# Two reordered fronts, early first expert pairs, and one block per layer in a macaron block with top-2 experts

## The chip, the cores and the metric

The kernel runs on one core of a Trainium2 chip. The time is the device time in microseconds (us) from the first to the last instruction of one execution. Five engines work side by side: TensorE (PE; its weight loads are PEld), VectorE (DVE), ScalarE (ACT), GpSimd (POOL) and SyncE (SP). Each takes its own instructions strictly in order and waits on semaphores; transfers run on 16 DMA engines, and SP, ACT and POOL issue them. Execution of a wait blocks everything behind it on the same engine.

## The reference, cut to what matters

Input x has 8 x 1024 tokens of 128 features in float32. Twice a layer of experts is applied with half weight, and attention stands between:

```python
x = x + 0.5 * ffn(layernorm(x))        # layer 0
x = x + attn(layernorm(x))             # linear attention, 16 heads of 8
x = x + 0.5 * ffn(layernorm(x))        # layer 1, the same weights

# ffn(xf): 16 experts, 2 of them for each token, and 1 shared one
scores = softmax(xf @ gate_w + gate_b)
top_vals, top_idx = top_k(scores, 2)
cw = (one_hot(top_idx, 16) * top_vals[..., None]).sum(axis=1)
a = silu(xf @ w1 + b1) * (xf @ w3 + b3)              # per expert, 128 -> 176
y = einsum('teh,ehd,te->td', a, w2, cw) + cw @ b2
z = silu(xf @ sw1 + sb1) * (xf @ sw3 + sb3) @ sw2 + sb2   # shared, 128 -> 352

# attn(xf)
q, k, v = xf @ Wq + bq, xf @ Wk + bk, xf @ Wv + bv   # split into heads
q, k = elu(q) + 1, elu(k) + 1
kv = einsum('bhnd,bhnf->bhdf', k, v)
out = einsum('bhnd,bhdf->bhnf', q, kv) @ Wp + bp
```

## The kernel before

The 8192 tokens are 64 tiles of 128 rows. A *group* is 8 tiles (1024 tokens), a *chunk* is 4 tiles (512 tokens), so there are 8 groups and 16 chunks. The residual stays in SBUF as `xa`. Five phases follow each other: front 0, experts 0, front 1, experts 1, combine. Each is one block of five engine programs and ends in `phase`, which clears its semaphores and makes all engines meet.

**A front** (`front`, n = 0 or 1) does for each group: layer norm (DVE `moments`, `variances`; the scale on DVE in front 0, on POOL in front 1; ACT `rows`), transposes on PE (`turn`) copied by ACT (`turned`), the gate's matmuls (`gating_mm`), the top two on DVE (`largest`, `indices`, `hot`), a count on PE with triangular ones (`count`), and from it on DVE each token's slot in its expert's region (`places`). POOL then sends each tile's normalised rows to the DRAM array `xs` by one indirect DMA a tile: `first(c)` for the first choice of a chunk, and after DVE has rewritten the row's tail (`rewrite(c)`, which waits until these sends have landed, `sent0`), `second_choice(c)`. Beside it runs the shared expert, six parts m for each group: PE `ups(m)` (6 matmuls of 512 columns), ACT `silus(m)`, DVE `gates(m)`, PE `downs(m)`, and per chunk DVE `outs`. PE's `ups(0)` needs the split weights `sw13l`, which DVE makes. Front 0 also splits the 16 experts' weights into a high and a low part through one PSUM buffer `p_w`: PE `weight_mean(e)`, ACT `weight_high(e)`, DVE `weight_low(e)`. Front 1 first adds what the experts wrote (`residual`, from `yt` loaded by SP) and does the attention (`attention`, `phi_q`, `phi_k`, `attended`) two groups ahead of the shared expert. Near the end `tables`, `table` and `tables_out` make the list of expert tiles, and SP copies 16 padding tiles.

The order of the work is written out by hand: `step(s)` in front 0 and `step_1(s)` in front 1 on each engine, with an `opening` in front 1. In front 0 the start was `step(-1)` and `step(0)`.

**The experts** (`experts`) take 72 pairs of tiles. SP loads pair j into `xin[j % 8]` once the slot's old rows are sent; for pair j PE transposes (`p_x`), multiplies with the two experts' weights (`p_u`), transposes `a` (`p_a`) and multiplies with `w2` (`p_y`); DVE scales into `y`, and POOL sends it to the DRAM array `ys` with two indirect DMAs a pair. PE's step j holds: transposes of pair j+1, up of pair j, transposes of `a` of pair j-1, down of pair j-2.

**Combine** adds `ys` to `xa` in 8 pieces of 1 MB (4 buffers) and stores 8 pieces of 0.5 MB.

```python
        front(nc, k, sb, ps, 0, xa, xs_dram, w)
        experts(nc, k, sb, ps, 0, xs_dram, ys_dram)
        front(nc, k, sb, ps, 1, xa, xs_dram, ys=ys_v)
        experts(nc, k, sb, ps, 1, xs_dram, ys_dram)
        combine(nc, sb, xa, ys_v, out_v)
```

## Time and profile before

| | us |
|---|---|
| median of 3 runs | 942.99 (941.9 to 943.26) |
| profiled execution | 942.32 |
| its span, first to last instruction | 940.6 |
| PE busy | 785.1 (83%) |
| DVE busy | 580.3 (62%) |
| POOL busy | 568.9 (60%) |
| ACT busy | 470.5 (50%) |
| mean granted TensorE clock, share of full | 0.94 |

The span outside the instructions is 942.32 - 940.6 = 1.7 us. In the trace front 0 runs from 0 to 215 us, experts 0 to 416, front 1 to 702, experts 1 to 905, and combine to the end. A row of the timeline reads: start in us, duration in us, engine, line of the kernel, operation, what it writes <- what it reads, how often, and in brackets how long its engine had stood idle and which engine, tile and line released it. "SPq" and "ACTq" are issues of DMAs by that engine.

### The profile page before, as it was taken

How to read it: one execution, taken by the hardware profiler on the slowest of the kernel's cores; microseconds unless marked ns; L12 is line 12 of the kernel's file. 1: busy time of each engine (PE TensorE's matmuls, PEld its weight loads, DVE VectorE, ACT ScalarE, POOL GpSimd, SP SyncE). 2: the span in 40 equal slices, each digit the busy share in tenths (PEclk: the TensorE clock that was granted, in tenths of full speed). 3: DMA queues.
4: the chain of work that ended last, by engine and by line, in shares of the span. 5: the costliest groups of instructions: out<-in, count | busy, mean ns of one | idle time of the engine just before them, and what ended most of it. 6: DMA issues, size and time to landing. Idle time of an engine off the chain costs nothing. (4 is left out here: it accounts for less than half of the span.)

```text
span 940.6 us, 20435 instructions
## 1 busy us (share of the span) xinstructions
PE 785.1 (83%) x5348; PEld 699.7 (74%) x5349; DVE 580.3 (62%) x2146; ACT 470.5 (50%) x968; POOL 568.9 (60%) x585
## 2 busy tenths in 40 slices
PE   2899999886999999936678999999868999999910
PEld 2577777666999999934567777787758999999900
DVE  7688786643555555537667877766634555555535
ACT  2465566423555555525457667675314555555500
POOL 1376777772777776751167667765643777776730
PEclk9999999997999999977889999999798999999965
DMA  9921221132333333324112211111133333333349
GB/s 279 157 65 55 70 70 59 52 98 66 102 101 101 104 101 101 100 97 145 65 32 83 76 39 46 35 38 35 43 81 81 108 101 104 101 101 98 93 185 376
DMA packets 83816, 90.45 MB, mean 96 GB/s; under 512 B 20391, under 2 KB 69421, under 8 KB 82733
## 3 DMA queue, kind: packets, MB, share of 16 engines
q1 hardware_dynamic: 64046, 45.41, 19.1%
q0 software_dynamic: 17408, 35.95, 11.4%
q10 hardware_dynamic: 2304, 8.39, 2.3%
q8 instruction: 27, 0.44, 0.2%
q14 instruction: 31, 0.25, 0.1%
HBM read 47.45 MB, written 44.37 MB: 98 GB/s over the span
## 5 line engine op out<-in xcount | busy, mean ns | idle before, releaser
L1415 POOL DMA_INDIRECT ys<-e_y,e_x x288 | 276.6, 960 | 134.4 <-issue 88.7
L354 POOL DMA_INDIRECT xs<-f_xrow,f_slot x256 | 261.1, 1020 | 128.0 <-issue 74.6
L1534 PE MATMUL e_py<-w,e_at 97*128 (+1 forms) x1152 | 152.1, 274 | 0.0
L1534 PEld LDWEIGHTS e_py<-w,e_at 97*128 97x128 f32 (+1 forms) x1152 | 139.9, 191 | 0.1
L1439 DVE TENSOR_TENSOR e_a<-e_pu,e_sil 128x352 f32<-128x352 f32 x144 | 75.6, 525 | 97.6 <-ACT e_sil L1465 97.6
L1446 DVE TENSOR_SCALAR e_y<-e_py,e_x 128x128 f32<-128x128 f32 x288 | 87.8, 347 | 57.6 <-PE e_py L1534 57.3
L1168 PEld LDWEIGHTS f_pz<-sw,f_gated 128*128 128x128 f32 (+1 forms) x768 | 101.6, 195 | 14.3 <-DVE f_gated L561 4.5
L1465 ACT ACTIVATE e_sil<-e_pu 128x352 f32<-128x352 f32 x144 | 67.0, 465 | 90.3 <-PE e_pu L1511 90.3
L1509 PE MATMUL e_pu<-w13h,e_xth 128*128 x288 | 107.2, 372 | 0.0
L1459 ACT ACTIVATE e_xth<-e_px 128x256 fp32r<-128x256 f32 x144 | 55.6, 386 | 101.0 <-PE e_px L1498 101.0
L1168 PE MATMUL f_pz<-sw,f_gated 128*128 128x128 f32 (+1 forms) x768 | 103.4, 279 | 3.0 <-DVE xa L571 2.9
L946 ACT ACTIVATE f_sil<-f_phg,sb 128x512 f32<-128x512 f32 (+1 forms) x96 | 65.3, 686 | 78.9 <-PE f_phg L1154 74.7
L561 DVE SCALAR_TENSOR_TENSOR f_gated<-f_phg,sb,f_sil 128x512 f32<-128x512 f32 (+1 forms) x96 | 71.5, 746 | 41.2 <-ACT f_sil L946 35.6
L1154 PE MATMUL f_phg<-f_xth,sw13h 128*128 128x512 f32 (+1 forms) x192 | 88.1, 459 | 8.4 <-ACT f_sil L946 6.4
L1510 PE MATMUL e_pu<-w13l,e_xth 128*128 x288 | 94.3, 327 | 0.0
L1511 PE MATMUL e_pu<-w13h,e_xtl 128*128 x288 | 94.2, 327 | 0.0
L1471 ACT ACTIVATE e_at<-e_pa 96x512 f32<-96x512 f32 x144 | 85.8, 596 | 1.6 <-PE e_pa L1521 1.6
L1521 PE MATMUL e_pa<-ident,e_a 128*96 128x128 f32 x576 | 86.2, 272 | 0.0
L1154 PE MATMUL f_phg<-f_xtl,sw13h 128*128 128x512 f32 (+1 forms) x192 | 77.6, 404 | 0.0
L1154 PE MATMUL f_phg<-f_xth,sw13l 128*128 128x512 f32 (+1 forms) x192 | 77.6, 404 | 0.0
L1498 PE MATMUL e_px<-ident,e_x 128*128 128x128 f32 x288 | 57.7, 282 | 21.2 <-DMA e_x<-xs 17.0
L1521 PEld LDWEIGHTS e_pa<-ident,e_a 128*96 128x96 f32 x576 | 67.2, 125 | 5.1
(168 smaller groups left out, 1320.2 us busy)
## 6 DMA issues: line engine op xcount, KB each, us to landing
e_x<-xs SPq DMA_DIRECT2D x288, 65.0 KB
f_yt<-ys SPq DMA_DIRECT2D x16, 512.0 KB, 4.1
c_yt<-ys SPq DMA_DIRECT2D x8, 1024.0 KB, 10.4
ys<-e_y,e_x POOLq DMA_INDIRECT x288
xa<-in_attn_x ACTq DMA_DIRECT2D x8, 512.0 KB, 9.8
xs<-f_xrow,f_slot POOLq DMA_INDIRECT x256, 2.4
out<-xa ACTq DMA_DIRECT2D x8, 512.0 KB
f_raw<-in_ffn_w SPq DMA_DIRECT2D x32, 88.0 KB
```

The costliest lines, as they stand in the source:

```text
L354: pool.indirect_dma_start(xs, bass.IndirectOffsetOnAxis(slot[:, q, i:i + 1], 0), xrow[:, i, :], None).then_inc(done, 16)
L1154: last = pe.matmul(p_hg[(2 * m + g) % NH][0:wd], w_[:, cols], x_[c % NX][:], start=q == 0, stop=q == 2)
L1168: last = pe.matmul(p_z[c % NZ][:, tok], gated[c % 2][0:wd, f, tok], k.sw2[0:wd, f], start=f == 0 and q == 0, stop=f == 2, skip_group_check ...
L1415: pool.indirect_dma_start(ys, bass.IndirectOffsetOnAxis(xin[r][:, t, D:D + 1].bitcast(I32), 0), y[r][:, t, :], None).then_inc(sent[r], 16)
L1439: dve.tensor_tensor(a[r][:], p_u[r][:, :, INTER:UP], sil[r][:], ALU.mult).then_inc(aa, 1)
L1446: last = dve.tensor_scalar(y[s][:, t], p_y[j % 2][:, t * D:(t + 1) * D], xin[s][:, t, D + 1:D + 2], None, ALU.mult)
L1471: act.activation(at[r][0:A0], p_a[0:A0], ACT.Copy).then_inc(turned, 1)
L1509: pe.matmul(o, xth[r][:, tok], k.w13h[:, cols], start=True, stop=False)
L1510: pe.matmul(o, xth[r][:, tok], k.w13l[:, cols], start=False, stop=False)
L1511: last = pe.matmul(o, xtl[r][:, tok], k.w13h[:, cols], start=False, stop=True)
L1521: last = pe.transpose(p_a[0:A0, q * P:(q + 1) * P], a[r][:, t, o:o + A0], k.ident[:])
L1534: last = pe.matmul(p_y[r][:, t * D:(t + 1) * D], at[r][0:rows_, q], w2, start=c == 0, stop=c == 1, skip_group_check=True)
```

## The change

1. The front and the experts of a layer are one block without a clearing and a meeting of the engines in between. Each engine goes on by itself, and waits for `ended`: all `outs` done, all sends landed, the table made (and in layer 0 the attention's weights). SP loads the first 4 pairs as soon as pads and sends have landed, before the other conditions. At the end of the experts SP loads the first 4 chunks of `ys` before the engines meet. The buffers of these loads, `k.xin` and `k.yt`, are now allocated for the whole program, and front 0's raw weights and front 1's `xt_a` lie in them.
2. Front 0 begins with an order of its own instead of `step(-1)` and `step(0)`. The odd experts' weight splits move from the end of step s to the second part of step s+1. `rewrite(2(s-1))` moves ahead of `gates(m + 1)`, `tables` behind `low`. SP, not ACT, loads the tokens of groups 3 to 7. ACT runs one early exponential on a constant.
3. Front 1: `phi_k` ahead of the two shifts in `features`, ACT's `exps(0)` behind `turned_a(5)`, and the count of step 7 one part later.
4. Experts: the down projection and the weighing of pair 0 stand at the end of step 1 instead of step 2.
5. Combine works in 16 chunks with 12 buffers.

```diff
+def load_x(nc, sp, k, n, xin, xs, first, pairs, free=None, turn=None):
+    _, at = nc.values_load_multi_w_load_instructions(
+        k.tile_at[0:1, ds(first, 2 * len(pairs))], engines=[mybir.EngineType.SP],
...
+    for q, r in enumerate(pairs):
+        if free is not None:
+            sp.wait_ge(free[r], turn)
+        for t in range(2):
+            sp.dma_start(xin[r][:, t], slot_rows(xs)[:, ds(at[2 * q + t], 1)].rearrange(
+                "p j c -> p (j c)")).then_inc(k.x_in[n][r], 16)
+def layer(nc, k, sb, ps, n, xa, xs, ys, ys_v, w=None):
+    with phase(nc) as sem:
+        with ExitStack() as ctx:
+            first, ended = front(nc, k, sb, ps, sem, ctx, n, xa, xs, w, ys_v)
+        with ExitStack() as ctx:
+            second = experts(nc, k, sb, ps, sem, ctx, n, xs, ys, ys_v, ended)
+            with nc.Block(no_gpsimd_drain=True) as block:
+                @block.sync
+                def _(sp):
+                    first[0](sp)
+                    second[0](sp)
...
@@ front, SP @@
             load_expert(3)
+            for g in range(3, GROUPS):
+                load_tokens(sp, g)
...
         sp.wait_ge(pads, 16 * E)
+        sp.wait_ge(sent1, 16 * TILES)
+        load_x(nc, sp, k, n, [k.xin[:, r] for r in range(AHEAD)], xs, 0, range(AHEAD))
...
@@ front 0, DVE step(s) @@
-                    gates(m + 1)
-                    outs(2 * (s - 1) - 1)
             rewrite(2 * (s - 1))
-                    gates(m + 2)
             if s == 1:
                 rewrite(1)
+            gates(m + 1)
+            if s <= GROUPS:
+                weight_low(2 * s - 1)
+            outs(2 * (s - 1) - 1)
+            gates(m + 2)
...
@@ front 1, DVE features(a) @@
             phi_q(a, 1)
+            phi_k(a, 0)
+            phi_k(a, 1)
             shifts(a - 1)
             shifts_a(a + 1)
-                    phi_k(a, 0)
-                    phi_k(a, 1)
...
@@ front 0, DVE after the memsets @@
-                    step(0)
+            largest(0)
+            indices(0)
+            hot(0)
+            sums(0)
+            places(0)
+            low(0)
+            low(1)
             dve.wait_ge(swhi, 1)
             dve.tensor_tensor(k.sw13l[:], raws[:], k.sw13h[:].bitcast(F32), ALU.subtract
                               ).then_inc(swlo, 1)
+            weight_low(0)
+            moments(2)
+            variances(2)
+            scales(2)
...
@@ front 1, ACT opening @@
             rows_a(4)
-                    exps(0)
-                    rows_a(5)
             turned_a(4)
-                    high(0)
+            rows_a(5)
             turned_a(5)
+            exps(0)
+            high(0)
             high(1)
...
@@ front 0, ACT start @@
-                    step(-1)
-                    step(0)
+            for c in range(2):
+                rows(c)
+                turned(c)
+            rows(2)
+            rows(3)
+            turned(2)
+            exps(0)
+            turned(3)
+            high(0)
+            high(1)
             act.wait_ge(sw_in, 32)
...
@@ front 0, PE step(s) @@
                 ups(m)
+                if i == 1 and n == 0 and s <= GROUPS:
+                    weight_mean(2 * s - 1)
                 downs(m - 2)
...
-                            if gating and n == 0:
-                                weight_mean(2 * s + 1)
...
@@ front 1, PE step_1(s) @@
-                        if i == (1 if s == 1 else 0) and gating:
+                if i == (1 if s in (1, GROUPS - 1) else 0) and gating:
                     count(s)
...
+    ended = [(outr, CHUNKS), (sent1, 16 * TILES), (tab_done, 1)]
+    if n == 0:
+        ended += [(bias, 2)]
...
@@ experts, SP @@
+        for done, value in ended:
+            sp.wait_ge(done, value)
+        load_x(nc, sp, k, n, xin, xs, 2 * AHEAD, range(AHEAD, RING))
         with sp.Fori(1, PAIRS // RING) as i:
...
+        for r in range(RING):
+            sp.wait_ge(sent[r], 32 * (PAIRS // RING))
+        for c in range(4):
+            load_y(sp, ys_v, c, k.yt[:, c], k.y_in[n][c])
...
@@ experts, PE step(j) (DVE the same with weigh) @@
-                    if 2 <= j:
+            if j == 1:
+                down_projection(2, 2)
+            if j > 2:
+                down_projection(j, jv)
...
@@ combine, SP @@
+                for c in range(4, CHUNKS):
+                    wait(sp, ysum, c - 11)
+                    load_y(sp, ys, c, yt[c % 12], in_ready[c])
```

Three places show how the rows of an engine's program move. First PE at the start of front 0, before (`f_pt` are transposes, `f_pg` the gate's matmuls and the count, `f_pw` a weight split, `f_phg` the first `ups`):

```order
L1132 MATMUL f_pt<-ident,f_xrow 128x128 x8
L1108 MATMUL f_pg<-gw_s,f_xt 128x16 x8
L1118 MATMUL f_pg<-f_mask,tri 128x128
...
L1176 MATMUL f_pw<-f_raw,f_centre 128x352
L1177 MATMUL f_pw<-f_rawb,f_part 128x352
L1132 MATMUL f_pt<-ident,f_xrow 128x128 x8
L1176 MATMUL f_pw<-f_raw,f_centre 128x352
L1177 MATMUL f_pw<-f_rawb,f_part 128x352
L1108 MATMUL f_pg<-gw_s,f_xt 128x16 x8
L1154 MATMUL f_phg<-f_xth,sw13h 128x512
```

and after:

```order
L1215 MATMUL f_pt<-ident,f_xrow 128x128 x8
L1191 MATMUL f_pg<-gw_s,f_xt 128x16 x8
L1215 MATMUL f_pt<-ident,f_xrow 128x128 x8
L1201 MATMUL f_pg<-f_mask,tri 128x128
...
L1259 MATMUL f_pw<-yt,f_centre 128x352
L1260 MATMUL f_pw<-yt,f_part 128x352
L1191 MATMUL f_pg<-gw_s,f_xt 128x16 x8
L1237 MATMUL f_phg<-f_xth,sw13h 128x512
```

The second eight transposes stand ahead of the count, and one weight split is gone from here. Second DVE in front 1's opening, before (`f_phq` and `f_phk` are `phi_q` and `phi_k`, `f_nm` and `f_nma` the two shifts, `xa<-xa,f_yt` the residual):

```order
L605 TENSOR_SCALAR f_vea<-f_mva 128x8
L617 SCALAR_TENSOR_TENSOR f_phq<-f_phq,f_phg 128x512 x2
L464 SCALAR_TENSOR_TENSOR f_nm<-f_mv,f_rs 128x8
L611 SCALAR_TENSOR_TENSOR f_nma<-f_mva,f_rsa 128x8
L622 SCALAR_TENSOR_TENSOR f_phk<-f_phk,f_phg 128x256 x2
L579 TENSOR_TENSOR xa<-xa,f_yt 128x512
```

and after:

```order
L671 TENSOR_SCALAR f_vea<-f_mva 128x8
L683 SCALAR_TENSOR_TENSOR f_phq<-f_phq,f_phg 128x512 x2
L688 SCALAR_TENSOR_TENSOR f_phk<-f_phk,f_phg 128x256 x2
L530 SCALAR_TENSOR_TENSOR f_nm<-f_mv,f_rs 128x8
L677 SCALAR_TENSOR_TENSOR f_nma<-f_mva,f_rsa 128x8
L645 TENSOR_TENSOR xa<-xa,yt 128x512
```

The two `f_phk` now stand ahead of the shifts, which need POOL's results. Third PE at the first pairs of the experts, before (`e_px` transposes of x, `e_pu` up, `e_pa` transposes of a, `e_py` down):

```order
L1511 MATMUL e_pu<-w13h,e_xtl 128x352
L1521 MATMUL e_pa<-ident,e_a 96x128 x4
L1498 MATMUL e_px<-ident,e_x 128x128 x2
...
L1511 MATMUL e_pu<-w13h,e_xtl 128x352
L1521 MATMUL e_pa<-ident,e_a 96x128 x4
L1534 ISA
L1534 MATMUL e_py<-w,e_at 128x128
```

and after:

```order
L1600 MATMUL e_pu<-w13h,e_xtl 128x352
L1610 MATMUL e_pa<-ident,e_a 96x128 x4
L1628 ISA
L1628 MATMUL e_py<-w,e_at 128x128
...
L1587 MATMUL e_px<-ident,xin 128x128 x2
```

The down projection of pair 0 follows the first transposes of `a` at once, ahead of the transposes and the up part of later pairs.

## Rows read from the trace of the kernel before

**Rows 1.** Stretches by --windows: engine busy us (instructions), PE clock, DMA share, GB/s.
```profile
472.00:701.00 229.00, 209.93 (x1300) 173.99 (x1300) 158.50 (x686) 137.75 (x282) 147.91 (x139) 0.96 0.17 52
908.00:935.00 27.00, 0.00 (x0) 0.00 (x0) 17.60 (x15) 0.00 (x0) 0.00 (x0) 0.50 1.00 410
```

**Rows 2.** Timeline of front 0's start, PE and DVE.
```profile
24.55 0.69 PE L1121 MATMUL f_pg<-f_mask,onesb 128*128 128x128 bf16 x8
...
29.15 0.28 DVE L516 TENSOR_TENSOR f_spot<-f_pg,f_base 128x128 f32<-128x128 f32 x1
...
30.93 1.45 DVE L550 TENSOR_TENSOR f_xtl<-f_xt,f_xth 128x512 fp32r<-128x512 f32 x2
...
35.05 0.89 DVE L885 TENSOR_TENSOR sw13l<-f_raws,sw13h 128x704 fp32r<-128x704 f32 x1 [0.15 <-ACT sw13h L1086]
...
36.00 3.59 PE L1108 MATMUL f_pg<-gw_s,f_xt 128*128 128x16 f32 x16 [2.16 <-DVE sw13l L885]
...
39.63 0.29 DVE L471 TENSOR_TENSOR f_lgt<-f_pg,gb_s 128x128 f32<-128x128 f32 x1 [3.61 <-PE f_pg L1108]
...
43.64 0.75 DVE L561 SCALAR_TENSOR_TENSOR f_gated<-f_phg,sb,f_sil 128x512 f32<-128x512 f32 x1 [1.08 <-ACT f_sil L946]
```

**Rows 3.** Timeline of front 0's steps: PE and POOL.
```profile
78.32 2.46 POOL L354 DMA_INDIRECT xs<-f_xrow,f_slot  x1 [5.29 <-DVE f_slot L532]
...
78.88 0.83 PE L1176 MATMUL f_pw<-f_raw,f_centre 128*128 128x352 f32 x2 [1.04 <-DVE w13l L642]
...
211.02 0.96 POOL L354 DMA_INDIRECT xs<-f_xrow,f_slot  x1 [0.30 <-issue]
```

**Rows 4.** The page's DMA issues: the sends of a front, median us to landing.
```profile
xs<-f_xrow,f_slot POOLq DMA_INDIRECT x256, 2.4
```

**Rows 5.** Timeline, SP's first loads for experts 0.
```profile
215.88 8.16 SPq L1402 DMA_DIRECT2D e_x<-xs  x16
```

**Rows 6.** Timeline of the first pairs of experts 0.
```profile
220.85 0.49 PE L1510 MATMUL e_pu<-w13l,e_xth 128*128 x1
...
225.12 0.59 ACT L1471 ACTIVATE e_at<-e_pa 96x512 f32<-96x512 f32 x1
...
226.56 1.06 PE L1534 MATMUL e_py<-w,e_at 97*128 x8
...
229.18 0.96 POOL L1415 DMA_INDIRECT ys<-e_y,e_x  x1 [17.20 <-DVE e_y L1446]
```

**Rows 7.** The page's groups: the same matmul over both experts' phases.
```profile
L1510 PE MATMUL e_pu<-w13l,e_xth 128*128 x288 | 94.3, 327 | 0.0
```

**Rows 8.** Timeline from experts 0 to front 1.
```profile
414.58 0.96 POOL L1415 DMA_INDIRECT ys<-e_y,e_x  x1 [0.30 <-DMA ys<-e_y,e_x]
417.86 27.91 SPq L297 DMA_DIRECT2D f_yt<-ys  x10
```

**Rows 9.** Timeline of front 1's opening, DVE and PE.
```profile
454.54 0.17 DVE L611 SCALAR_TENSOR_TENSOR f_nma<-f_mva,f_rsa 128x8 f32<-128x8 f32 x1 [1.29 <-POOL f_rsa L381]
...
455.09 1.22 PE L1246 MATMUL f_pb<-f_phk,f_v 128*128 128x128 f32 x4 [4.51 <-DVE f_phk L622]
```

**Rows 10.** Timeline of front 1's step 7.
```profile
665.90 0.29 PE L1118 MATMUL f_pg<-f_mask,tri 128*128 128x128 bf16 x1 [2.00 <-DVE f_mask L504]
...
669.54 0.75 DVE L561 SCALAR_TENSOR_TENSOR f_gated<-f_phg,sb,f_sil 128x512 f32<-128x512 f32 x1 [2.70 <-PE f_phg L1154]
```

**Rows 11.** Timeline from front 1 to experts 1.
```profile
695.50 0.96 POOL L354 DMA_INDIRECT xs<-f_xrow,f_slot  x1 [0.30 <-issue]
...
700.72 0.69 DVE L571 SCALAR_TENSOR_TENSOR xa<-f_pz,xa 128x512 f32<-128x512 f32 x1 [1.87 <-PE f_pz L1168]
...
704.31 9.39 SPq L1402 DMA_DIRECT2D e_x<-xs  x16
706.82 0.69 PE L1498 MATMUL e_px<-ident,e_x 128*128 128x128 f32 x2 [6.15 <-DMA e_x<-xs]
```

**Rows 12.** Timeline, the last addition of combine.
```profile
935.77 1.23 DVE L1574 TENSOR_TENSOR xa<-xa,c_yt 128x1024 f32<-128x1024 f32 x1
```

More of the change, by code:

```diff
@@ L50 @@
 RING = 8
+AHEAD = 4
 SENT_EARLY = 3
@@ L1552, in combine @@
-def combine(nc, sb, rs, ys, out):
-    with phase(nc) as sem, ExitStack() as ctx:
-        yt = [sb(f"c_yt{r}", [P, GT, 2 * D], ctx=ctx) for r in range(4)]
-        in_ready = [sem(f"c_in{r}") for r in range(GROUPS)]
+            gates(m)
+            if attending:
+                moments(f)
+            gates(m + 1)
+            if attending:
+                variances(f)
+            outs(2 * (s - 1) - 1)
+            if gating:
+                sums(s)
+                places(s)
+            if s == GROUPS - 1:
+                tables()
@@ new lines, in step_1 @@
+            if gating:
+                low(2 * s + 1)
+        if n == 0:
+            for r in range(4):
+                dve.memset(rawb[r][:], 0.0)
+            dve.memset(k.w2[0:32, 1], 0.0)
+            dve.memset(rawp[:], 0.0)
+            dve.memset(rowq[:], 0.0).then_inc(zeroed, 1)
+            moments(0)
+            variances(0)
+            scales(0)
+            shifts(0)
+            moments(1)
+            variances(1)
+            scales(1)
+            shifts(1)
+        for r in range(2):
+            dve.memset(gated[r][96:97, 2], 1.0)
@@ L1557, in combine @@
+def combine(nc, k, sb, rs, ys, out):
+    with phase(nc) as sem, ExitStack() as ctx:
+        yt = [k.yt[:, c] for c in range(4)]
+        yt += [sb(f"c_yt{r}", [P, CHUNK, 2 * D], ctx=ctx)[:] for r in range(8)]
+        in_ready = k.y_in[1] + [sem(f"c_in{c}") for c in range(4, CHUNKS)]
         half, ysum, stored = sem("c_half"), sem("c_ysum"), sem("c_stored")
```

2568 lines of the change are left out of this document (1278 added, 1290 removed).

## The prediction

> **What bounds the kernel now.** I read the share of busy time first, then the timeline around each phase's two ends, then who waits for whom inside a phase. Three things are to be seen. In the experts POOL sets the pace: from its first send to its last it needs 414.58 - 229.18 = 185.4 us for 143 intervals, 1.30 us each, of which 0.96 is the send and 0.30 the gap behind it [rows 6, 8]. In front 0 POOL is as near the bound as PE: it waits 5.29 us for the slots of group 2 at 78.32 [rows 3], and from there to 211.02 its 99 intervals take 132.7 us, 1.34 each or 21.4 a group of 16 sends, with hardly a wait. In front 1 PE is the bound, busy 209.93 of 229 us [rows 1]. Combine is bound by the DMA engines: share 1.00 at 410 GB/s [rows 1]. Between these phases nothing runs but landings, meetings and loads: 215.88 - 211.98 = 3.9 us from the end of POOL's last send of front 0 to the experts' first load [rows 3, 5], and 706.82 - 701.41 = 5.4 us from DVE's last work to PE's first at the second front's end [rows 11].
>
> The sum is made against the profiled execution of 942.32 us (span 940.6, 1.7 outside it), which is 0.7 below the median of 942.99.
>
> **Front 0, its start: -4.9.** PE's first full step begins at 36.00, released by DVE's `sw13l` (35.05 + 0.89 = 35.94) [rows 2]. In the new order DVE has only this between the end of the count (24.55 + 0.69 = 25.24) and `sw13l`: `places`, which takes 1.4 of the 1.8 us from 29.15 to 30.93 (the rest is a weight split), `low` for two chunks 1.45, and `sw13l` 0.89: 25.24 + 1.4 + 1.45 + 0.89 = 29.0. ACT and PE keep up in my count: the four transposes and copies end by 24.1, `high` and `sw13h` by 26. So PE starts its step 6.9 earlier. Not all of it carries. DVE now does a weight split (0.5) and moments, variances and scale of group 2 (about 4.6; most of what lay between 24.3 and 29.15) before the top two of group 1, so that these start at 34.1 and not 39.63, and the first `gates` behind ACT's silu come at 38.2 and not 43.64: -5.45. From there `weight_mean(2s-1)`, 1.6 us of PE (two rows of 0.8 as at 78.88 [rows 3]), stands between `ups(m+1)` and `ups(m+2)`, ahead of the count and the slots. It takes back up to 1.6 in each step, and PE's wait of 1.04 at 78.88 goes with the split that made it, as does DVE's work for that split. The two nearly cancel: no gain a step, and POOL's 21.4 stay the measure. Slots of group 2 come 4.5 to 5 earlier, and POOL from its send at 78.32 needs 211.02 - 78.32 us whatever PE does. Hence -4.9, with ends 0 (POOL gives it back) and -8 (7 waits of about 1.0 are gained too, until POOL's own pace stops it). Cover that could go: `rewrite(2(s-1))` now waits for sends that land 2.4 us after their issue [rows 4], before `gates(m+1)`. Four sends at 1.27 and the landing put it 7.6 us behind POOL's first send of the group, and the rest of DVE's step to the next slots is some 12 us by my count of its instructions: 20.4 with the 0.8 to POOL's start, less than POOL's 21.4, so it costs nothing; were it 2 us more, each of six steps would lose 1. The moved token loads cost nothing: group 3's are wanted near 40 us.
>
> **From front 0 to experts 0: -1.8.** The last send lands at 211.02 + 2.4 = 213.4 [rows 3, 4], and SP's first load goes out at 215.88 [rows 5]. The clearing, the meeting and 16 register loads lie between, 2.5 us. With SP waiting for the landing alone and loading 8 registers, I leave 0.6 to 0.7. That is -1.8; ends: -0.8 (register loads take the full 1.0 and more) and -2.5.
>
> **The first pairs: +0.7, twice.** PE runs without a gap here. The down part of pair 0 now waits for ACT's copy, which ends at 225.12 + 0.59 = 225.71, some 0.75 us after PE's transposes; before, PE used that time for pair 2 and came to it at 226.56 [rows 6]. So `y` of pair 0 is ready 0.8 earlier, and everything from pair 1 on 0.75 later. POOL, back to back from 229.18, starts 0.8 earlier but then waits for pair 1. PE, without a gap and at POOL's pace, does not catch up. I take +0.7 each; ends -0.8 (the early start is kept) and +0.8.
>
> **From the experts on: -0.8, twice.** 417.86 - (414.58 + 2.4) = 0.9 us lie between the last landing and the first load of `ys` [rows 8]; SP now loads right behind the landing. The trace shows no landing for these sends; I use the front's 2.4 [rows 4]. The same holds before combine. Ends 0 and -1.3 each.
>
> **Front 1: -1.4 and -2.4.** In the opening DVE waits 1.29 us for POOL's scale at 454.54, ahead of `phi_k`, and PE stands 4.51 us for `phi_k` [rows 9]. Moved ahead, `phi_k` starts 1.4 earlier, and the chain behind it (attention, moments, top two) has no gap to swallow that. What ACT's `exps(0)` frees for PE ends in DVE, which is busy: 0 more. In step 7 PE stands 2.00 us for the mask at 665.90, and then DVE 2.70 for `ups(37)` [rows 10]. The six matmuls now fill PE's wait. The count comes 1.5 to 2 us later but still ahead of `gates(37)`: -2.4 for the slots of group 7, on which POOL, the rewrites and the tail hang. Ends: 0 and -6.
>
> **From front 1 to experts 1: -5.3, and -1.5 for the clock.** DVE's last `outs` ends at 701.41, PE's first expert matmul starts at 706.82 [rows 11]. The last send of this front lands at 695.50 + 2.4 = 697.9, so the first load goes out at 698.5, and its data come 706.82 - 704.31 = 2.5 us later, at 701.0, ahead of `outs`. PE starts at 701.5. It has hardly stood still then, and before, it ran its first pairs at the lower clock: a matmul took 0.49 us at 220.85 against 0.327 in the mean [rows 6, 7]. Twelve such ahead of the first `y` give 12 x 0.16 = 1.9; I take 1.5. Ends -4 and -7.5 together.
>
> **Combine: -1.5.** Bytes and rate stay. What shrinks is the tail: two additions of 1.23 us [rows 12] become half, -1.2, and the last store (940.6 - 937.0 = 3.6 us behind them) is half as large, for which I take 0.3; ends 0 and -3. The row has the DMA share at 1.00 with four pieces of 1 MB queued, and I expect the same rate of twelve smaller ones. Against this stands the Trainium skill, page "DMA: Bandwidth & Descriptors", section "Bandwidth": batch DMAs to 1 MiB or more for 75% of peak (341 GB/s for 1 MB, 425 for 16 MB). The trace has stores of 0.5 MB in the full rate already, but loads of 1 MB; none of halves of both.
>
> Sum: -4.9 - 1.8 + 1.4 - 1.6 - 3.8 - 5.3 - 1.5 - 1.5 = -19.0. 942.32 - 19.0 = 923.3, and 924.0 as a median.
>
> **Rivals.** (1) Only the ends count: DVE and POOL give back what the reordered fronts win. For it: POOL and PE are equally near the bound, and a step has a weight split more on its critical part. Against: both waits named in front 1 stand on the chain. Then -4.9 and -3.8 fall out: 932.7. (2) More than forecast: the early first pair is kept (-0.8 instead of +0.7, twice: -3.0), and front 0 gains one wait more. For it: POOL lags PE by several sends at the end of the experts, so that PE's lead grows in any case. Against: PE's gapless rows. 920. (3) Combine slows with small pieces. If each piece costs so much that the rate falls by a fifth of the 27 us at 410 GB/s [rows 1], 5.4 us: 929.4. Against: the full DMA share. By the two rates that the Trainium skill's page "DMA: Bandwidth & Descriptors" gives in "Bandwidth", a fifth is also the most that it would be. (4) Slower than before: TensorE stays at the lower of its two levels for a stretch of front 1. There the clock's mean is 0.96 [rows 1], and a matmul costs half as much again or more at the lower level (0.49 against 0.327). PE's 21 us a group become about 32, so two further groups at the lower level cost 22 us and turn -19 into +3: 946. For it: the reordering moves PE's waits, and the clock had fallen before 665.90 already. Against: the change takes PE's gaps away rather than adding any.
>
> **How the numbers follow.** Forecast (924, itself 920 to 928) 0.52, rival 1 0.22, rival 2 0.15, rival 3 0.06, rival 4 0.03, the rest 0.02. The range, 8 in 10: from 917.5 (rival 2 with the ends of the boundary terms) to 934 (rival 1 and a little more). About 0.2%, 1.9 us, is what a measurement can tell: faster by more than that 0.95, within it 0.02, slower 0.03.
>
> **What would show it.** PE's first `ups` near 32.5 us, the send that now waits at 78.32 near 73.4, POOL's last send of front 0 near 206, SP's next load under 1 us behind its landing. The down part of pair 0 behind a PE wait of 0.7, and POOL's second pair later than 2.53 us behind the first. No PE wait of 2 us at the count of step 7. At front 1's end less than 1 us between the last `outs` and PE's first expert matmul, which runs at the full clock. Over 400 GB/s in combine. The forecast is wrong if front 0's last send is still near 212, if the loads ahead of the meeting are not earlier, or if a phase of the experts takes over 188 us from first to last send.

## The result, and the profile after

| | before | after |
|---|---|---|
| median of the runs shown | 942.93 (941.9 to 943.26, 4 runs) | 938.15 (935.98 to 940.38, 4 runs) |
| profiled execution, span | 942.32, 940.6 | 940.38, 938.3 |

The ratio is 0.9955, 95% interval 0.9936 to 0.9974: faster by 4 to 5 us, where 19 were forecast and 917.5 to 934 was the range. All times below are us. The two profiled executions differ by less, 2.3, and where this time went is read from milestones that both traces have:

| stretch | before | after | change | forecast |
|---|---|---|---|---|
| start to POOL's last send of front 0 | 211.02 | 217.19 | +6.2 | -4.9 |
| to the first load of experts 0 | 4.86 | 3.05 | -1.8 | -1.8 |
| to the last send of experts 0 | 198.70 | 201.00 | +2.3 | +0.7 |
| to the slots of group 0 in front 1 | 62.73 | 61.23 | -1.5 | -0.8 - 1.4 |
| to the slots of group 7 | 196.12 | 192.56 | -3.6 | -2.4 |
| to POOL's last send of front 1 | 22.07 | 22.09 | 0 | 0 |
| to the first load of experts 1 | 8.81 | 3.44 | -5.4 | -5.3 |
| to the first send of experts 1 | 13.17 | 12.08 | -1.1 | -1.5 |
| to the last send of experts 1 | 185.46 | 187.77 | +2.3 | +0.7 |
| to the end of the span | 37.66 | 37.89 | +0.2 | -0.8 - 1.5 |

(Slots are DVE's `f_slot` rows, eight in each front, groups 0 to 7; those of front 1 begin at 477.31 and end at 673.43 before, 482.47 and 675.03 after.) The column of changes sums to -2.3, the difference of the two spans. The profiled execution of after is the slowest of its four; three later kernels with the same front 0 had its last send at 215.3 to 215.6 and not 217.19, so some 1.7 of the +6.2 is likely chance.

**Front 0's start.** The timeline of step 1, of POOL, DVE and PE (start, duration, engine, line, tiles, in brackets the idle time before it and what ended it):

```profile
27.70 1.22 POOL L421 DMA_INDIRECT xs<-f_xrow,f_slot  x1 [23.51 <-DVE f_slot L598]
...
38.03 0.75 DVE L627 SCALAR_TENSOR_TENSOR f_gated<-f_phg,sb,f_sil 128x512 f32<-128x512 f32 x1 [1.02 <-ACT f_sil L1021]
44.51 0.17 DVE L608 SCALAR_TENSOR_TENSOR f_xrow<-f_rec,f_wtop 128x4 f32<-128x4 f32 x1 [5.72 <-DMA xs<-f_xrow,f_slot]
...
45.56 0.95 POOL L421 DMA_INDIRECT xs<-f_xrow,f_slot  x1 [7.80 <-DVE f_xrow L610]
...
50.47 0.17 DVE L608 SCALAR_TENSOR_TENSOR f_xrow<-f_rec,f_wtop 128x4 f32<-128x4 f32 x1 [5.72 <-DMA xs<-f_xrow,f_slot]
...
51.51 0.77 PE L1237 MATMUL f_phg<-f_xth,sw13h 128*128 128x512 f32 x1 [7.38 <-DVE f_gated L627]
```

Up to 38.03 all is as forecast (first send 27.70, first gates at 38.0; the forecast had 38.2, and [rows 2] has 43.64). Then DVE comes to `rewrite(0)`, which may not touch `xrow` before the first sends have read it, and stands 5.72; `rewrite(1)` right behind costs 5.72 more. L627 at 50.62, the gates on which PE waits, stands behind both. Sends that were to land in 2.4 [rows 4] took far longer. The DMA issues of the first 60 us (KB each, median from issue to landing), and SP's queue. The 10.6 is the median of the four landings that the trace has, those of the sends issued from 33.02 to 36.80:

```profile
xs<-f_xrow,f_slot POOLq DMA_INDIRECT x16, 10.6
xs<-pad_tail SPq DMA_DIRECT2D x1, 32.0 KB, 26.6
```

```profile
18.12 11.00 SPq L341 DMA_DIRECT2D xs<-pad_tail  x1
29.16 12.05 SPq L355 DMA_DIRECT2D w<-in_ffn_w  x2
```

And the windows (start:end, length, busy us and count of PE, PEld, DVE, ACT, POOL, then granted clock, DMA share, GB/s):

```profile
28.00:32.00 4.00, 3.21 (x15) 3.21 (x16) 3.78 (x21) 0.31 (x1) 3.09 (x4) 1.00 1.20 219
32.00:36.00 4.00, 4.00 (x11) 2.88 (x11) 3.41 (x29) 0.41 (x2) 3.08 (x4) 1.00 1.55 80
36.00:40.00 4.00, 1.95 (x6) 1.34 (x6) 1.73 (x13) 2.55 (x4) 1.46 (x2) 0.85 1.49 54
```

By queue, 36 to 40 (packets, MB, share of the 16 engines; q0 has POOL's sends, q1 what SP issued):

```profile
q0 software_dynamic: 86, 0.20, 82.6%
q1 hardware_dynamic: 1341, 0.01, 66.4%
```

The share adds up the times of all packets, so it can pass 1. A share of 1.5 that moves 54 to 80 GB/s is mostly the 4096 tails of 8 bytes, the second of the two writes of padding rows: SP's 1341 packets carry 0.01 MB, some 8 bytes each, and POOL's 86 packets beside them take 82.6% of the engines' time (in e9_pads_split, where the tails are gone, 79 packets take 10.5% in the same 4 us). The tails pass just when POOL sends its first eight tiles. Before the change they passed at 28 to 32 (share 1.61 at 31 GB/s), ahead of the sends, and DVE asked for the landings only at 45.39. The Trainium skill, page "DMA: Bandwidth & Descriptors", section "Specifications", gives 512 B as the least transfer at line rate and says that below it a DMA does a read-modify-write; the low rate agrees, the mechanism no trace here shows. Its section "Issuing engines are not separate DMA queues" says that transfers started by SP, ACT and GpSimd run on the same 16 engines and interleave; the sends' 10.6 us beside SP's write agree with that.

**Ends of front 0, and the first pairs.** POOL's last send, SP's first load, then PE and POOL in experts 0:

```profile
217.19 0.96 POOL L421 DMA_INDIRECT xs<-f_xrow,f_slot  x1 [0.30 <-issue]
...
220.24 4.03 SPq L159 DMA_DIRECT2D xin<-xs  x8
...
229.06 1.03 PE L1610 MATMUL e_pa<-ident,e_a 128*96 128x128 f32 x4
230.86 1.15 PE L1628 MATMUL e_py<-w,e_at 97*128 x8 [0.77 <-ACT e_at L1560]
...
235.18 1.06 PE L1628 MATMUL e_py<-w,e_at 97*128 x8
...
237.79 0.95 POOL L1497 DMA_INDIRECT ys<-e_y,xin  x1 [2.00 <-DVE e_y L1534]
241.36 0.96 POOL L1497 DMA_INDIRECT ys<-e_y,xin  x1 [1.35 <-DVE e_y L1534]
```

Before, PE's first matmul of the experts and its transposes of `a` of pair 0:

```profile
218.38 0.69 PE L1498 MATMUL e_px<-ident,e_x 128*128 128x128 f32 x2 [10.81 <-DMA e_x<-xs]
...
224.49 0.60 PE L1521 MATMUL e_pa<-ident,e_a 128*96 128x128 f32 x4
```

The first load follows 3.05 behind the last send, against 4.86 [rows 3, 5]. The down part of pair 0 begins 7.98 behind PE's first matmul (222.88); before it was 8.18 [rows 6]. So the early place wins 0.2 and not 0.8. ACT's copy is waited for (0.77), as forecast, and it comes later than forecast, because the four transposes ahead of it take 1.03 where they took 0.60: the granted clock is 0.52 in 228 to 230 and 1.00 from 230 on, and before it was 0.89 in 224 to 226 and 1.00 behind that. The full clock came 7.0 behind PE's first matmul and not 6.1. That is not the new order's doing: in e4_pairs_old, which has the old order, it also comes 7.0 behind. The down part itself ran at the full clock. The down part of pair 1 begins 12.30 behind that start instead of 10.70, and POOL's third pair 7.79 behind its first instead of 5.42: 2.4 lost, 3 times the forecast.

**From the experts to front 1.**

```profile
423.55 6.76 SPq L165 DMA_DIRECT2D yt<-ys  x5
...
426.89 0.24 POOL L414 IOTA f_xrow<- 128x64 int32 x1 [4.69 <-POOLq L74]
...
427.42 1.03 DVE L933 MEMSET f_gated<- 1x512 f32 x2 [11.82 <-PEq L74]
...
428.54 0.69 DVE L645 TENSOR_TENSOR xa<-xa,yt 128x512 f32<-128x512 f32 x1
```

SP issues its first load 2.31 behind the last send, 0.97 earlier than before [rows 8]. But L74 is the meeting, and it ends 5.65 behind the last send of 421.24 (POOL's row at 426.89) where it ended 3.3 behind it: SP issues four loads before it comes to the meeting. DVE's first addition no longer waits for data; it stands behind the meeting and its own memsets, 7.30 behind the last send against 7.37. Further on in the opening PE's wait for `phi_k` is 3.01 where it was 4.51 [rows 9], and DVE's wait for POOL's scale (462.27) stands behind it:

```profile
461.29 0.71 PE L1329 MATMUL f_pb<-f_phk,f_v 128*128 128x128 f32 x4 [3.01 <-DVE f_phk L688]
```

**Step 7 and the end of front 1** (PE, DVE, SP, PE):

```profile
671.32 0.23 PE L1201 MATMUL f_pg<-f_mask,tri 128*128 128x128 bf16 x1 [1.27 <-DVE f_mask L570]
...
675.03 0.18 DVE L598 CAST f_slot<-f_at 128x16 int32<-128x16 f32 x1
...
700.56 3.98 SPq L159 DMA_DIRECT2D xin<-xs  x8
...
703.12 0.41 PE L1587 MATMUL e_px<-ident,xin 128*128 128x128 f32 x2 [0.89 <-DMA xin<-xs]
```

PE's wait for the mask is 1.27 instead of 2.00, DVE's of 2.70 is gone [rows 10]; the slots of group 7 follow 19.7 behind those of group 6 instead of 23.2. The windows from the one to the other, before and after:

```profile
650.28:673.43 23.15, 20.46 (x116) 17.63 (x115) 12.72 (x54) 12.35 (x22) 15.96 (x16) 0.78 0.14 47
655.32:675.03 19.71, 17.43 (x118) 14.86 (x117) 12.66 (x55) 12.31 (x22) 14.42 (x15) 1.00 0.14 48
```

The granted clock was 0.78 there before, and 1.00 after. So the 3.4 are not all the new order's: e11_before_split, which has the order of before, needs 21.6 at a clock of 0.84. No run has that order at the full clock, and how the 3.4 divide stays open. PE starts the experts 0.2 behind the end of the last `outs` (702.27 + 0.69), and not 5.4 [rows 11]; its first transposes take 0.41 where they took 0.69.

**Combine.** DVE's first addition, and two windows:

```profile
906.74 0.69 DVE L1670 TENSOR_TENSOR xa<-xa,yt 128x512 f32<-128x512 f32 x1 [12.22 <-DMA yt<-ys]
```

```profile
910.00:915.00 5.00, 0.00 (x0) 0.00 (x0) 3.61 (x7) 0.00 (x0) 0.00 (x0) 0.50 0.95 332
915.00:935.00 20.00, 0.00 (x0) 0.00 (x0) 14.91 (x22) 0.00 (x0) 0.00 (x0) 0.50 1.04 413
```

Then the stretch from the first addition to the last landing, before and after:

```profile
910.87:934.51 23.64, 0.00 (x0) 0.00 (x0) 17.11 (x15) 0.00 (x0) 0.00 (x0) 0.50 1.00 410
906.74:933.81 27.07, 0.00 (x0) 0.00 (x0) 20.55 (x30) 0.00 (x0) 0.00 (x0) 0.50 1.02 394
```

From the last send the first addition comes after 6.33 (7.93 before), and from the last landing (933.81) to the end it takes 4.49 (6.09 before): both ends are 1.6 shorter. What lies between is 3.4 longer. By the windows 10.7 MB (27.07 x 394) pass between these marks and not 9.7 (23.64 x 410): with smaller pieces, bytes that used to pass at the ends pass in the middle, some 2.4 us at 410 GB/s. The other 1 us is the lower mean rate: 332 GB/s in the hole at 910 to 915, and 413 behind it.

### The profile page after: what moved, and what is told of

It is laid out like the page before. It is cut to its first block and busy times, and to the rows that moved or that the text cites. A ratio compares the mean times of both kernels' runs of the same rounds, so it can differ in the third digit from the quotient of the medians.

```text
span 938.3 us, 20437 instructions
## 1 busy us (share of the span) xinstructions
PE 789.3 (84%) x5348; PEld 702.2 (75%) x5349; DVE 582.3 (62%) x2162; ACT 469.9 (50%) x969; POOL 562.5 (60%) x585
## 5 line engine op out<-in xcount | busy, mean ns | idle before, releaser
L421 POOL DMA_INDIRECT xs<-f_xrow,f_slot x256 | 255.3, 997 | 135.5 <-issue 69.6
L1497 POOL DMA_INDIRECT ys<-e_y,xin x144 | 137.9, 958 | 87.5 <-DVE e_y L1534 45.6
L1497 POOL DMA_INDIRECT ys<-e_y,e_x x144 | 137.9, 958 | 43.9 <-issue 42.4
L627 DVE SCALAR_TENSOR_TENSOR f_gated<-f_phg,sb,f_sil 128x512 f32<-128x512 f32 (+1 forms) x96 | 71.3, 746 | 36.8 <-ACT f_sil L1021 35.3
L1515 DVE SCALAR_TENSOR_TENSOR e_xtl<-e_px,e_xth 128x256 fp32r<-128x256 f32 x144 | 60.1, 418 | 13.5 <-ACT e_xth L1548 13.4
```

Source lines behind the costliest of these rows:

```text
L421: pool.indirect_dma_start(xs, bass.IndirectOffsetOnAxis(slot[:, q, i:i + 1], 0), xrow[:, i, :], None).then_inc(done, 16)
L627: dve.scalar_tensor_tensor(gated[c % 2][0:wd, f], p_hg[(2 * m + 1) % NH][0:wd], k.sb13[0:wd, 1, f:f + 1], sil[m % 2][0:wd], ALU.add, ALU.m ...
L1497: pool.indirect_dma_start(ys, bass.IndirectOffsetOnAxis(xin[r][:, t, D:D + 1].bitcast(I32), 0), y[r][:, t, :], None).then_inc(sent[r], 16)
```

## The experiments

All ratios are against runs of the kernel before on the same chip. "Waits" are DVE's two for landings in step 1 (L608, 27 to 60), "last send" is POOL's last of front 0, both in the profiled run.

| kernel | waits | last send | median | ratio, 95% interval |
|---|---|---|---|---|
| before | 0 | 211.02 | | 1 |
| after | 11.4 | 217.19 | 938.15 | 0.9955 (0.9936 to 0.9974) |
| e2_rewrite_back | 6.5 | 212.70 | 935.73 | 0.9916 (0.9891 to 0.994) |
| e3_tokens_act | 7.7 | 213.09 | 936.65 | 0.9925 (0.9905 to 0.9945) |
| e1_pads_last | 0.2 | 211.86 | 936.18 | 0.9916 (0.9898 to 0.9934) |
| e5_pad_rows | 5.1 | 208.81 | 930.41 | 0.9863 (0.9838 to 0.9888) |
| e8_rows_back | 0 | 207.07 | 929.55 | 0.9845 (0.9821 to 0.9869) |
| e9_pads_split | 0.3 | 205.87 | 928.54 | 0.9845 (0.982 to 0.9871) |
| e11_before_split | 0 | 212.26 | 942.13 | 0.9986 (0.997 to 1.0002) |
| e4_pairs_old | 10.6 | 215.41 | 935.62 | 0.9916 (0.9895 to 0.9937) |
| e6_one_load | 10.5 | 215.56 | 939.66 | 0.9951 (0.9933 to 0.997) |
| e7_big_pieces | 9.5 | 215.34 | 939.35 | 0.9958 (0.994 to 0.9976) |
| e10_best | 0 | 207.31 | 925.01 | 0.9822 (0.9791 to 0.9854) |
| e12_final | 0.2 | 205.79 | 924.93 | 0.9792 (0.9774 to 0.981) |

**e1_pads_last**

```
+ (behind the loop over load_expert(4..15))
  sp.wait_ge(tail, 2)
  sp.dma_start(rows[:, :, 0:D], k.zero ...)      # 2 MB of zeros
  sp.dma_start(rows[:, :, D:ROW], k.pad_tail[:]) # 8-byte tails
```

> The changed kernel, with the two writes of padding rows (2 MB of zeros, and the 8-byte tails) issued behind the last expert's weights instead of ahead of w2. Theory A: in step 1 of front 0 DVE stands 5.7 + 5.7 us ahead of rewrite(0) and rewrite(1) because the padding writes fill the DMA engines when the first eight sends go out. Then both waits go (under 1 us each), the slots of group 1 come near 52 instead of 61.9, POOL's last send of front 0 near 207 instead of 217, and the time is 928 to 930. Theory B: the sends land late because w2 and the other loads stand in the same queues, or because eight sends in a row are slow by themselves: then the waits stay above 8 us together and the time stays at 936 to 939. Against both: if the padding writes are slow wherever they stand, they reappear as waits of the sends or of the table later, and the time is above 935 though step 1 has no wait.

The group of L608 (busy, mean ns, idle before), then the late writes and DVE's wait, and a window between them:

```profile
L608 DVE SCALAR_TENSOR_TENSOR f_xrow<-f_rec,f_wtop 128x4 f32<-128x4 f32 x3 | 0.5, 160 | 0.2 <-DMA xs<-f_xrow,f_slot 0.2
```

```profile
147.96 0.42 SPq L356 DMA_DIRECT2D xs<-zero  x1
148.42 8.27 SPq L358 DMA_DIRECT2D xs<-pad_tail  x1
...
174.62 0.17 DVE L608 SCALAR_TENSOR_TENSOR f_xrow<-f_rec,f_wtop 128x4 f32<-128x4 f32 x1 [6.66 <-DMA xs<-f_xrow,f_slot]
```

```profile
165.00:170.00 5.00, 2.77 (x15) 2.22 (x16) 1.91 (x15) 3.19 (x6) 3.78 (x5) 1.00 1.36 66
```

Both halves of the question in one run. In step 1 the waits are gone and the slots of group 1 come at 51.24 (61.86 in after). Where the padding now stands, at 148 to 170, the same thing happens: share 1.36 at 66 GB/s, a wait of 6.66 for landings, and the slots of group 7 come 27.9 behind those of group 6, against 21 to 22 for groups 2 to 6. So the time is 936, and the padding is shown to be a cause by being moved with its effect. One thing moved with it: the loads of `w2` (1.4 MB), which stand behind the padding in SP's queue, are issued from 17.7 to 22.1 here and from 29.2 to 41.2 in after. At 148 to 170 they play no part.

**e2_rewrite_back**

```
  gates(m)
- rewrite(2 * (s - 1)); if s == 1: rewrite(1)
  gates(m + 1); weight_low(2 * s - 1); outs(2 * (s - 1) - 1)
+ rewrite(2 * (s - 1))
  gates(m + 2)
+ if s == 1: rewrite(1)
```

> The changed kernel, with rewrite(2(s-1)) and rewrite(1) of front 0 back where the kernel before has them (behind gates(m+1) and outs, and behind gates(m+2)). Theory B (the order is the cause: the sends landed no earlier before, DVE just asked later): DVE's gates of step 1 no longer stand behind the landings, the slots of group 1 come near 53 and the time is 928 to 931. Theory A (the landings themselves are late, 44.4 and 50.4): DVE still has to wait for both before hot(1), only two gates run earlier, the slots of group 1 come at 59 to 62 and the time is 935 to 938.

Nearer to theory A, and its time: DVE still waits 6.5 for the landings. But only `hot(1)` and what follows stands behind that, so the slots of group 1 come at 57.66, 1.3 ahead of A's range; in four kernels with the changed order (after, e4, e6, e7) they come at 59.96 to 61.86, without the wait at 51.24. The order is worth 2 to 4 us, the landings the rest.

**e3_tokens_act**

```
- for g in range(3, GROUPS): load_tokens(sp, g)
- for g in range(3): load_tokens(act, g)
+ for g in range(GROUPS): load_tokens(act, g)
```

> The changed kernel, with all eight token loads on ACT's queue at the start, as before the change. Theory C (the five token loads moved onto SP's queue push the padding writes and w2 back by about 6 us, into the first sends): the padding's issue takes 7.3 us again instead of 11.0, the sends of group 0 land by 39 and 44, the waits of 5.7 and 5.7 shrink to under 3 together, time 929 to 932. Theory A: the padding writes still stand ahead of the sends, the waits shrink by 2 to 4 us at most, time 934 to 938. A token load of group 0 or 1 that comes later for it would make the start later by 1 to 2 us.

```profile
L606 DVE SCALAR_TENSOR_TENSOR f_xrow<-f_rec,f_wtop 128x4 f32<-128x4 f32 x2 | 0.3, 167 | 7.7 <-DMA xs<-f_xrow,f_slot 7.7
```

The waits fall from 9.5 to 11.4 (four kernels with this front) to 7.7. The moved token loads, 2.5 MB ahead of the padding in SP's queue, are a fifth to a third of the stall. Theory C as the whole cause has fallen; theory A's 2 to 4 fits.

**e4_pairs_old**

```
- if j == 1: down_projection(2, 2)     (PE; DVE: weigh(2, 2))
- if j > 2: down_projection(j, jv)
+ if j >= 2: down_projection(j, jv)
```

> The changed kernel, with the down part and the weighing of pair 0 back in step 2 of the experts, as before the change. By the traces a phase from first load to last send took 198.7 before and 201.0 now (experts 0), so the early down of pair 0 costs 2.3 us a phase: 4.6 in all, time 933.5 to 934, POOL's second pair 2.5 us behind the first. By my prediction it costs 0.7 a phase: 936.7. If the 2.3 come from the loads now split in two lots of eight (the second lot waits for front's last outputs), nothing changes: 938.

```profile
232.29 0.96 POOL L1497 DMA_INDIRECT ys<-e_y,xin  x1 [15.93 <-DVE e_y L1532]
237.76 0.96 POOL L1497 DMA_INDIRECT ys<-e_y,xin  x1 [0.73 <-DVE e_y L1532]
```

POOL's third pair again comes 5.47 behind its first. From first to last send the two phases take 185.4 and 185.1, against 187.7 and 187.8 in after: 2.3 and 2.6 each. From the first load the gain is 1.8 in experts 0 (199.2 against 201.0), since the first send is 0.5 later. The early down part costs what the traces had said, and the rival of the split loads has fallen. The median fell by 2.5 and not by 4.6: in the profile of e4 front 1 needs 3.0 more from the slots of group 0 to those of group 7 than in after, for 1.6 of which e12_final below has the reason.

**e5_pad_rows, e8_rows_back, e9_pads_split**

```
  e5: pad_rows = xrow[:, TILES - PADS:, :]     (used by groups 4 to 7 only later)
      pool.memset(pad_rows, 0.0); iota into pad_rows[:, :, D]
-     the writes of zeros and of tails
+     sp.dma_start(rows, pad_rows)             # 4096 rows of 520 bytes
      ACT, DVE and POOL wait for it before they fill xrow for group 4
  e8: e5 and the edit of e2_rewrite_back
  e9: e5 with the write in four parts, behind load_expert(4), (5), (6) and (7);
      they are issued at 31.20, 41.66, 47.83 and 63.00
```

> The changed kernel; the padding is written at its old place, but as 4096 whole rows of 520 bytes in one transfer, out of the part of xrow that groups 4 to 7 use later, instead of 4096 rows of 512 bytes and then 4096 tails of 8 bytes. Theory A1 (the 8-byte tails are what clogs the DMA engines: they took from SP's issue at 18.1 until 44.7 to land, with a DMA share above 1 at 54 to 80 GB/s): the share stays near 1 at over 150 GB/s, the eight first sends land by 38, both waits of DVE in step 1 are under 1 us, POOL's last send of front 0 comes near 206.5, time 926 to 929. Theory A2 (the 2 MB of padding in short rows do it, whatever the tails): the waits shrink by less than half, last send at 211 to 214, time 932 to 936.

> e5_pad_rows with the rewrites of front 0 back at the places of the kernel before. It asks whether rewrite(2(s-1)) ahead of gates(m+1), costed at nothing in my prediction, is free once the sends land in time. If so, within 1 us of e5_pad_rows (POOL's last send of front 0 within 1 us). If the early rewrites gain (POOL's second sends never wait), it is 1 to 3 us slower than e5; if they cost a little in each step because DVE comes to them before the landing, it is 1 to 3 us faster.

> e5_pad_rows, but the whole-row padding goes out in four parts of 0.5 MB, one behind each of the loads of experts 4 to 7 (after about 50 us), where the DMA engines are two thirds idle. Theory A (what stands in the DMA engines in 27 to 50 us delays the first sends, and nothing else makes the early rewrites wait): as in e1_pads_last the waits of DVE in step 1 are under 1 us together, and without e1's late clog POOL's last send of front 0 comes at 206 to 207, which is what my prediction gave for the whole front; time 926.5 to 928.5. Rival: the parts slow the sends of groups 1 and 2 instead, and the early rewrites wait there: last send at 208 to 210, time 929 to 931.

Of e5_pad_rows the group of L617 (the rewrite), the issue of the padding, and one window:

```profile
L617 DVE SCALAR_TENSOR_TENSOR f_xrow<-f_rec,f_wtop 128x4 f32<-128x4 f32 x2 | 0.3, 168 | 5.1 <-DMA xs<-f_xrow,f_slot 5.1
```

```profile
xs<-f_xrow SPq DMA_DIRECT2D x1, 2080.0 KB, 21.7
```

```profile
32.00:36.00 4.00, 4.00 (x11) 3.01 (x11) 3.41 (x29) 0.40 (x2) 3.08 (x4) 1.00 1.21 129
```

Of e9_pads_split the same group, a window, and POOL's waits for the slots of group 2 and its last send:

```profile
L619 DVE SCALAR_TENSOR_TENSOR f_xrow<-f_rec,f_wtop 128x4 f32<-128x4 f32 x3 | 0.5, 161 | 0.3 <-DMA xs<-f_xrow,f_slot 0.3
```

```profile
36.00:40.00 4.00, 2.37 (x9) 1.40 (x8) 2.62 (x18) 2.55 (x3) 1.71 (x3) 1.00 0.12 35
```

```profile
73.84 1.07 POOL L424 DMA_INDIRECT xs<-f_xrow,f_slot  x1 [6.59 <-DVE f_slot L609]
...
205.87 0.95 POOL L424 DMA_INDIRECT xs<-f_xrow,f_slot  x1 [0.30 <-issue]
```

Whole rows halve the waits (5.1), more than theory A2 allowed and less than A1 asked. All else stands in its place in e5, so the split into 512 bytes and a tail is half of the stall. The four sends issued from 33 to 37 say the same: they land after 10.6 (median) in after, 7.2 in e5, 3.3 in e9 and 2.3 in e1. Of the other half, 2 MB of whole rows and `w2` behind them are the cause together; the runs don't divide it, since e9, as e1, also lets `w2` out early (issued from 17.6 to 22.1, in e5 from 18.2 to 37.1). Nor was the padding of e9 out of the way altogether: the parts did not wait until 50, and the first 0.5 MB ran beside the first sends. The DMA share in 32 to 36 was 0.86 at 224 GB/s then, and DVE's waits came to 0.3. And then the forecast of front 0 comes true: "the send that now waits at 78.32 near 73.4, POOL's last send of front 0 near 206" reads 73.84 and 205.87 here. The early rewrites are worth something only then: with whole rows at the old place they cost 1.7 (e5 against e8), with the padding out of the way they gain 1.4 (e9 against e10_best, whose front 0 differs in this alone). These are single profiles (e12_final, with the rewrites early, repeats the last send at 205.79), and the medians of e5 and e8 lie within each other's runs. The rival of waits in groups 1 and 2 has fallen: the last send comes at 205.87, not at 208 to 210.

**e11_before_split**

> The kernel before the change, with the padding as in e9_pads_split and nothing else. If the padding was in nobody's way there (no DVE or POOL wait named a landing in its step 1), time unchanged, 942 to 944: then the padding costs only together with the change's early rewrites and early start. If it was hidden in before too (w2 and the weights of experts 4 to 7 come earlier), up to 2 us faster.

Before the change the padding, and `w2` behind it, cost nothing that shows: the interval holds 1. The 10 us between after and e9_pads_split (1.1% by the ratios) are a cost that the change itself uncovered.

**e6_one_load, e7_big_pieces**

```
  e6: for c in range(1): load_y(...)     (was range(4)), the rest behind the meeting
  e7: combine: 6 loads of 1 MB for 12 of 0.5 MB, 8 stores for 16
```

> The changed kernel, but only the first of the four loads of ys stands ahead of the meeting behind the experts, in both layers; the other three follow behind it. Theory: SP reaches the meeting only after it has issued all four (1.75 us), so the meeting ends 1.3 us later than it could and takes back what the early load won. Then POOL's iota behind experts 0 comes 4.4 us after the last send instead of 5.65, POOL's first scale 9.4 after it instead of 10.6, and of front 1's opening 1.2 us is won; from the last send of experts 1 to the end it stays at 37.9 or falls by up to 1. Time 935.5 to 937. Rival (the landings of the loads set the pace, not the meeting): 10.6 and 938 stay.

> The changed kernel; combine's last twelve loads of 0.5 MB are six of 1 MB, its sixteen stores of 0.5 MB eight of 1 MB, as in the kernel before; the four early loads stay. From the last send of experts 1 to the span's end the kernel before took 37.7 us, the changed one 37.9, though its first addition comes 1.6 us earlier. Theory P (smaller pieces lower the rate, 414 GB/s against 423 between 915 and 935): the rate goes back to 420 or more, the last addition is 0.7 us earlier, and the longer tail (two additions of 0.7 and half a store more) takes as much: 37.5 to 38.5. Theory Q (the hole is at 910 to 915, 332 GB/s, because the next loads are issued only behind the meeting, and the pieces don't matter): rate unchanged at 414, the tail alone is longer, 38.5 to 39.5.

e6_one_load, POOL behind its last send at 419.38; and e7_big_pieces, combine's full stretch:

```profile
423.60 0.24 POOL L414 IOTA f_xrow<- 128x64 int32 x1 [3.27 <-POOLq L74]
428.76 1.05 POOL L448 TENSOR_TENSOR f_rsa<-f_vea,nhalf 128x4 f32<-128x4 f32 x1 [4.76 <-DVE f_vea L671]
```

```profile
911.00:931.00 20.00, 0.00 (x0) 0.00 (x0) 14.83 (x23) 0.00 (x0) 0.00 (x0) 0.50 1.01 423
```

e6: the meeting ends 4.2 behind the last send (5.65), POOL's first scale comes 9.4 behind it (10.6), as the theory had it, but the later loads are later too, and DVE waits for one (0.70 at 429.31). The slots of group 0 come 60.78 behind the last send; the kernels with four early loads have 60.3 to 61.3, so nothing of the 1.2 is seen there. In combine one load is too few: 40.5 from the last send to the end against 37.9, outside what was expected. On the whole nothing is gained.

e7: after's stores are of 0.25 MB and e7's of 0.5 MB, half of what the expectations of e7 and e12 call them. The rate is 423 where after has 413, both some 14 to 34 behind the last send, so larger pieces went with 2.4% more (the rule of 1 MiB in the Trainium skill, page "DMA: Bandwidth & Descriptors", section "Bandwidth", points this way, with a far smaller effect). That the size alone sets the rate is not shown: the kernel before, with pieces of the same sizes and four buffers, has 410. The last store is twice as large and gives the gain back: 3.77 from the last addition to the end instead of 3.05, 38.3 in all.

**e10_best, e12_final**

```
  e10: split padding; rewrites and first pairs at their old places; one early load
       ahead of front 1, four ahead of combine; front 1's memsets and copy of base
       behind residual(2)
  e12: e10 with the rewrites early; combine: loads of 1 MB, stores of 0.5 MB
```

> All that the runs so far point to: padding as in e9_pads_split, rewrites of front 0 and the experts' first pairs at the places of the kernel before, only one load of ys ahead of the meeting behind experts 0, and front 1's memsets and its copy of base behind DVE's third residual addition. Front 0's last send at 206 to 207.5 (the rewrites' place is worth under 1 us once the sends land in time; if the early rewrites had gained, it is 208 or more here), 185.2 us from first to last send in each experts' phase instead of 187.7, front 1's first slots 1 to 1.5 earlier than 61.2 behind the last send of experts 0. Time 921 to 924. If the terms overlap (POOL or the clock takes them back), 924 to 927.

> e10_best with the rewrites of front 0 at the changed kernel's early places again, and in combine the last twelve loads of 0.5 MB as six of 1 MB, the stores left at 0.5 MB. By e9_pads_split against e10_best the early rewrites are worth 1.4 us once the sends land in time: last send of front 0 at 205.9, against 207.3. In combine the larger loads should keep the rate of e7_big_pieces (423 GB/s) and the small last store its tail (3.1 us behind the last addition instead of 3.7): 37.3 from the last send to the end instead of 37.9; if the rate was the stores' doing, 37.9 stays. Time 922.5 to 924.

e10: last send 207.31, 185.5 and 185.3 from first to last send in the two experts' phases, and the slots of group 0 in front 1 come 59.65 behind the last send of experts 0, where after needs 61.23 and e9 61.00. 925.01 is 1.0 above the range expected for it and in the range of its overlap. e12: last send 205.79, and combine takes 37.4 from the last send to the end, both as expected; the median is 924.93 against a kernel before of 944.36, above the 922.5 to 924 expected. Its profiled front 1 needs 31.2 us from the slots of group 1 to those of group 2 where e10 needs 29.6; e3 and e4 show the same 31.2, after and e9 the 29.6. The windows of this stretch, e10 and then e12:

```profile
494.00:524.00 30.00, 27.66 (x180) 23.08 (x179) 23.65 (x104) 20.20 (x43) 21.73 (x19) 1.00 0.22 72
494.00:524.00 30.00, 26.97 (x159) 21.72 (x158) 22.18 (x98) 18.85 (x40) 20.55 (x19) 0.94 0.22 72
```

The granted clock goes with it: in e12 it was at the lower of its two levels, 0.50, from 500.7 to 504.1, and 3.4 us at half speed are about the 1.6 that is lost. The traces of e3 and e4 have such a stretch at the same place, those of after, e9 and e10 have none. What brings it on in some kernels stays open. e12_final beats both kernels, by 2.1% against before (interval 1.9 to 2.3%); it is not told apart from e10_best, whose interval overlaps.

## Why the prediction was wrong

**The step that failed** is this one of front 0: "`rewrite(2(s-1))` now waits for sends that land 2.4 us after their issue [rows 4], before `gates(m+1)` ... so it costs nothing", with its neighbour "The moved token loads cost nothing" (by e3_tokens_act they are a fifth to a third of the stall). The 2.4 is a median over the program. The sends of group 0 took 10.6 (the four landings on record), since the padding was under way and `w2` behind it. The row for it stood in the profile of before (share 1.61 at 31 GB/s in 28 to 32, SP's issue of the tails 7.26 us long), but no instruction waited on it there. Nor did the sends land in 2.4 before the change: the packets of the first eight (32 each, 256 in all; 184 of them start before 44) end at 45.86 in that trace, 5.0 behind the eighth issue at 40.88, and DVE came to the rows of the last four only at 46.87. The change moved three things onto one spot: the sends 3.85 earlier, the tails later (2.5 MB of tokens ahead of them), and DVE's wait from behind 45.39 to 38.8. This cost 11.1 against the forecast of the term (-4.9 to +6.2); e9_pads_split, without it, is at 205.87, -5.15. The median of e9, 928.54, lies within the forecast's range. The rest of that term's working was right: PE's first `ups` at 32.23 (forecast 32.5), no net gain in the later steps. In the profiles the front's 11.1 are two thirds of what is missing (-2.3 for -19.0); the first pairs are 3.2 of it, combine 2.5, the way to front 1 0.7, and front 1 gave 1.2 more than forecast.

**The first pairs** were right in mechanism and mis-sized: the down part is behind a PE wait of 0.77 (0.7 forecast), and POOL waits for pair 1, but a phase loses 2.3 and not 0.7, beyond the upper end of 0.8. I had pair 0 ready 0.8 earlier; it is 0.2, in the main because the transposes ahead of it took 1.03 and not 0.60 at the lower clock, which lasted 1.0 longer here. And I took the loss as that of one wait, where pair 1 comes two steps of PE behind pair 0. e4_pairs_old shows the whole sum. The clock is no part of it: the second phase loses the same 2.3.

**From the experts to front 1** I priced SP's queue and forgot the meeting behind it: SP issues 0.97 earlier, all others leave the meeting 2.4 later, net -0.1 for the -0.8. e6_one_load shows the meeting move. **Combine** (-0.8 and -1.5, measured +0.2): both ends shrank by 1.6 each, and the middle gave it all back. The forecast said that bytes and rate stay, and still counted the shorter ends as won; 2.4 of the 3.4 are bytes that only moved from the ends into the middle. The other 1 is the mean rate, 394 against 410 GB/s. What makes the hole at 910 to 915 stays open; e12_final wins 0.5 of it.

**Right:** the end of front 0 (-1.8), the opening (-1.4), front 1 to experts 1 (-5.3, measured -5.4), the clock (-1.5, -1.1), and step 7 with 1.2 more than forecast, in which the clock has a part (0.78 to 1.00). None of the rivals named the stall of front 0. Rival 1 said that only the ends count, but in front 1 the opening paid in full and step 7 at least in part; rival 3 had the direction of combine's mean rate, at a fifth of its size; rival 4 did not come in after, but e3, e4 and e12 show it small, 1.6 us for 3.4 us at the lower level. Its price was read off wrongly: 21 us a group is front 0's pace, and front 1 needs 29.6. The "cover that could go" was looked at for a full step and not for step 1, and the range had no room for it.
